# Issuing one of four small row DMAs from ScalarE's queue, and six stack DMAs without a gap

## What is computed

```python
logits = einsum('bhqd,bhkd->bhqk', q, k) * scale      # causal mask added
attn = softmax(logits)
out = einsum('bhqk,bhkd->bhqd', attn, v)
for l in range(2):
    x = x + attention(ln(x))
    x = x + (token_moe, seq_moe)[l](ln(x))
```

## Time and profile before

| what | us |
|---|---|
| median of 3 runs | 1255.74 (1254.58 to 1256.5) |
| profiled execution, its own time | 1253.16 |
| its span, first to last instruction | 1251.4 |
| TensorE busy in the span | 1060.6 (85%) |
| VectorE busy | 980.6 (78%) |
| ScalarE busy | 792.0 (63%) |
| GpSimd busy | 685.8 (55%) |

### The profile page before, as it was taken

How to read it: one execution, slowest core, us unless ns; L and a number is a source line. 1 busy time by engine, 2 the same in 40 slices (tenths; PEclk the granted TensorE clock), 3 DMA queues, 4 the chain that set the end, 5 groups by cost and what they waited for, 6 DMA issues and landing times. The chain is left out here.

```text
span 1251.4 us, 37899 instructions
## 1 busy us (share of the span) xinstructions
PE 1060.6 (85%) x10453; PEld 789.4 (63%) x10453; DVE 980.6 (78%) x2919; ACT 792.0 (63%) x1908; POOL 685.8 (55%) x1018
## 2 busy tenths in 40 slices
PE   1788999999999999999369997388889889989997
PEld 0565666666666666666269997255656556658986
DVE  3678999999998898899547765368888998876665
ACT  1566777777777767776158886256666666754554
POOL 3345555556656777776723333566676676532332
PEclk9999999999999999999679999589999899989999
DMA  5232111111111221121122222243311212100000
GB/s 144 86 110 78 50 38 42 51 52 53 53 40 45 68 66 52 55 66 43 36 72 67 69 67 74 57 116 99 85 53 53 64 39 67 53 2 10 23 18 21
DMA packets 118053, 73.07 MB, mean 58 GB/s; under 512 B 8384, under 2 KB 112960, under 8 KB 117952
## 3 DMA queue, kind: packets, MB, share of 16 engines
q1 hardware_dynamic: 99296, 53.11, 15.3%
q10 hardware_dynamic: 14560, 10.35, 3.0%
q0 software_dynamic: 4096, 8.40, 2.1%
HBM read 21.68 MB, written 11.60 MB: 27 GB/s over the span
## 5 line engine op out<-in xcount | busy, mean ns | idle before, releaser
L617 DVE TENSOR_REDUCE negm<-bank 128x2 f32<-128x512 f32 (+1 forms) x576 | 389.3, 679 | 82.0 <-PE bank L309 57.0
L505 ACT ACTIVATE prob<-bank 128x512 f32<-128x512 f32 x576 | 339.6, 595 | 127.1 <-PE bank L331 88.8
L898 POOL TENSOR_SCALAR_AFFINE_SELECT prob<-prob 128x512 f32<-128x512 f32 x384 | 248.6, 649 | 172.6 <-ACT prob L505 170.7
L350 PE MATMUL bank<-prob,vaug 128*32 128x256 f32 (+1 forms) x3072 | 168.6, 338 | 4.1 <-ACT oT L511 3.3
L1217 POOL COPY w_job<-w_s 128x512 f32 x104 | 69.1, 665 | 153.4 <-PE bank L1186 152.6
L317 PE MATMUL bank<-stack 126*128 126x256 bf16 x768 | 151.8, 279 | 0.0
L336 PE MATMUL bank<-stack 128*128 128x256 bf16 x768 | 150.8, 278 | 0.9 <-ACT prob L505 0.9
L1208 ACT ACTIVATE prob<-bank,b_job 128x128 f32<-128x128 f32 (+1 forms) x416 | 131.8, 400 | 17.2 <-PE bank L1186 9.9
L1197 PE MATMUL bank<-w_job,prob 128*128 128x128 f32 x1088 | 139.0, 276 | 2.5 <-issue 1.6
L1197 PEld LDWEIGHTS bank<-w_job,prob 128*128 128x128 f32 x1088 | 131.3, 192 | 6.4 <-issue 5.3
L350 PEld LDWEIGHTS bank<-prob,vaug 128*32 128x32 f32 x3072 | 81.5, 110 | 80.7 <-issue 48.9
(11 more groups left out here) (181 smaller groups left out, 2122.0 us busy)
## 6 DMA issues: line engine op xcount, KB each, us to landing
stack<-parts SPq DMA_DIRECT2D x288, 128.0 KB
w_s<-e_w ACTq DMA_DIRECT2D x32, 256.0 KB, 3.0
oT<-x_routed SPq DMA_DIRECT2D x72, 64.0 KB, 1.7
y_routed<-oT SPq DMA_DIRECT2D x36, 128.0 KB, 1.9
stack<-mT SPq DMA_DIRECT2D x192, 4.0 KB
out<-x_all SPq DMA_DIRECT2D x16, 128.0 KB, 1.8
b_all<-e_b ACTq DMA_DIRECT2D x2, 512.0 KB, 8.4
x_routed<-hk,x_at POOLq DMA_INDIRECT x64
```

Of the source, the lines that this page charges most:

```text
L350: m = nc.tensor.matmul(o, w, (prob0, prob1)[kb][:, g % 2, h], start=kb == 0, stop=kb == 1, skip_group_check=True)
L505: nc.scalar.activation(o, s, ACT.Exp, scale=SCALE).then_inc(exp_done, 1)
L617: nc.vector.tensor_reduce(o, s, AX.X, ALU.max, negate=True).then_inc(max_done, 1)
L898: nc.gpsimd.affine_select(out=t, in_=t, compare_op=ALU.is_ge, fill=0.0, base=0, pattern=[[0, HG], [1, P]], channel_multiplier=-1).then_inc ...
```

## The change

In slot 2 of phases two and three, the row of group 1 is issued by ScalarE's queue, right after the second of the three exponentials of the slot, and SP issues the six stack DMAs of the next sample in a run. In phase one nothing is moved. The waits of the row (`mT_sb`, `sT_ps`) go with it. All other rows stay with SP.

```diff
+        def row(eng, i, g):
+
+            eng.wait_ge(mT_sb, 4 * i.v + g + 1)
+            alone(eng)
+            need(eng, sT_ps, 12 * (i.v - 2) + 3 * g + 3)
+            alone(eng)
+            eng.dma_start(stack[SHIFT:P, i.par, HG * g:HG * (g + 1), 0],
+                          mT[:, g % 2, :]).then_inc(row_dma[g % 2], 16)
+
@@ act_slot
             if ie:
                 act_exp(ie, ge, 1)
+            if k == 2 and im and im.phase > 0:
+                row(act, im, gm)
             if k == 1 and nxt:
                 act_part(nxt)
@@ sp_slot
+            by_act = k == 2 and im and im.phase > 0
             if k == 2 and nxt:
-                sp_stack(nxt, range(0, 2))
-            if im:
-                sp.wait_ge(mT_sb, 4 * im.v + gm + 1)
-                alone(sp)
-                need(sp, sT_ps, 12 * (im.v - 2) + 3 * gm + 3)
-                alone(sp)
-                sp.dma_start(stack[SHIFT:P, im.par, HG * gm:HG * (gm + 1), 0],
-                             mT[:, gm % 2, :]).then_inc(row_dma[gm % 2], 16)
-            if k == 2 and nxt:
-                sp_stack(nxt, range(2, 6))
-            if k == 3 and nxt:
-                sp_stack(nxt, range(6, TERMS))
+                sp_stack(nxt, range(TERMS if by_act else 2))
+            if im and not by_act:
+                row(sp, im, gm)
+            if k == 2 and nxt and not by_act:
+                sp_stack(nxt, range(2, TERMS))
```

## The result

| | median us | runs | ratio to before, 95% interval |
|---|---|---|---|
| before | 1255.16 | 1250.76 to 1256.5 (4) | 1 |
| changed | 1279.7 | 1274.61 to 1283.44 (4) | 1.0195 [1.0165, 1.0224] |

The change makes the kernel 2% slower, 24.5 us by the medians. The forecast was 1250.3. The profiled execution of the changed kernel took 1280.74 us, its span is 1279.0.

What follows compares the result with a forecast made beforehand. In phases two and three neither TensorE nor VectorE is full; they wait for each other. The terms 2.4 + 3.0 + 0 = 5.4 us gave 1255.74 - 5.4 = 1250.3 us, range 1244.5 to 1257.5.

Steps and rivals of the forecast that it cites:

- rival C: Phases two and three: the unbroken stack burst delays the row; 1265.3 us at a flight of 3.4 us; chance 0.12.
- When the row goes out: Row behind ScalarE's second exponential: leaves 0.3 us earlier in phase two; a 2.4 us flight holds even for late exponentials.
- the late second exponential: Exponential at 954.29 after late score matmuls, row needed at 957.43: with a flight of 2.4 us, 0.6 us left.
- I read the difference as queueing that a row on another queue mostly escapes: Row behind two stack DMAs: 3.74 us in phase three's sample with loads, 2.36 in the ordinary one; another queue mostly avoids this.
- The row leaves SP: ScalarE's extra issue of 0.34 to 0.66 us fits in its 0.83 us idling in the slot: priced at nothing.
- What it is worth in phase two: Earlier row in phase two: taken as 0, since VectorE sets the sample's length; at most 4.9 us.
- What it is worth at 835.86: Phase three sample with expert loads: row leaves earlier, removing 2.81 us of idling; gain 2.4 us, bounds 1.0 and 2.8.
- SP issues six in a run: SP's issue gap goes, so TensorE's stack waits in phases two and three shrink: 3.0 us, bounds 0 and 3.9.
- rival A: The transfers, not SP's issue, set the stack's landing, so the gap is worth 0: 1254.7 us, chance 0.24.
- a sign of being wrong: TensorE's granted clock in phase three, 0.96 before, moving by more than a hundredth would count against the forecast.

Runs made afterwards that it cites:

- e15: Kernel before, but the row goes out on SP behind three stack DMAs, with three behind it: 1273.95 us, ratio 1.0160.
- e5: Changed kernel, but SP issues two stack DMAs, waits until ScalarE has issued the row, then issues four: 1262.4 us, ratio 1.0066.
- e11: Changed kernel, but SP issues three stack DMAs, waits until ScalarE has issued the row, then issues three: 1273.9 us, ratio 1.0153.
- e4: Kernel before, plus an extra 4 KB DMA on ScalarE's queue in slot 2, where the change has the row: 1260.0 us, ratio 1.0043.
- e6: Kernel before, plus an extra 4 KB DMA on ScalarE's queue in slot 3: 1261.1 us, ratio 1.0063.
- e7: The change in phase three alone, phase two as in the kernel before: 1264.6 us, ratio 1.0100.
- e8: Kernel before, row on SP, but SP holds the four stack DMAs behind the row until it has landed: 1309.2 us, ratio 1.0440.
- e2: Kernel before, but the row goes out on SP behind four stack DMAs, with two behind it: 1311.4 us, ratio 1.0465.

## Why the prediction was wrong

The forecast (faster by 5.4 us) failed, and rival C, to which I gave 0.12, came: the row is delayed, L331 waits for it in nearly every sample, and the stages grow by what it waits.

- **"When the row goes out"** is the step that failed. Its first half held in phase two: 0.25 us behind the second exponential instead of 0.1, so 0.15 us sooner than from SP instead of 0.3. The second half, "with a flight of 2.4 us this holds", didn't: 3.5 in phase two. I took the flight from a row that had two stack DMAs ahead and moved the row, without asking what would be ahead of it then. In the kernel before, SP's own queue keeps the third stack DMA behind the row. Afterwards SP issues the third 1.38 us after the first, and ScalarE's row leaves at 1.69: it has become the fourth DMA instead of the third, and 128 KB more are ahead of it. e15, e5 and e11 show that this place is what counts, on whichever of the two queues. For the late second exponential, 954.29 in the prediction, I had counted 0.6 us to spare. In the changed kernel nine rows of phase three are that late, have four stack DMAs ahead, and land at 5.8 to 6.2 us.
- **"I read the difference as queueing that a row on another queue mostly escapes"** fell with it. The Trainium skill's rule (DMA: Bandwidth & Descriptors, Issuing engines are not separate DMA queues), that DMAs of all issuing engines run on the same DMA engines and that a second issuer saves no more than the time of initiating, agrees with e5, e11 and e15. The interleaving that the prediction quotes with it didn't help the row: its packets on ScalarE's queue moved only when the stack DMAs issued earlier were nearly through. I had weighed the rule for one sample of phase three, at 0.7 us; in the other 30 samples it changes the sign.
- **"The row leaves SP", at nothing:** not quite right. The third exponential starts up to 0.41 us late, L534 still idles, but an extra DMA of this size costs 5 to 7 us in e4 and e6, which I can place only in part.
- **"What it is worth in phase two", 0:** the slack was smaller still than the 0.2 us that I read. The landing grew by 0.9 to 1.0 us, and the sample by 13.8/15 = 0.92.
- **"What it is worth at 835.86", 2.4:** the mechanism held (e7); measured 1.8, since the stack landed 8.7 us after its first DMA, where I had allowed 8.0.
- **"SP issues six in a run", 3.0:** the issue became 0.7 us shorter (5.02 to 4.33). In the changed kernel the stack waits went from 0.6 + 3.3 to 1.8 in all (the 0.6 is gone). But TensorE was late by then for the row, which hides such waits. The landings that the traces record for the stack show the term by itself: the last of the six goes out 0.94 us sooner after the first in phase two and 1.0 us in phase three, but all have landed only 0.1 us sooner (7.78 us after the first issue for 7.90, medians) and 0.3 us (7.64 for 7.95). I had taken 0.7 from two samples of phase one. With 0.9 us of transfer for each 128 KB against 0.67 us of issue, the premise of rival A was right: the transfers set the pace. The Trainium skill (DMA: Bandwidth & Descriptors, Why a DMA increments its semaphore by 16 and not by 1) has such copies on 8 of 16 engines; the busy share of 0.50 to 0.57 in the run, after a first stretch of 0.7, agrees. By the same rule the row, two partitions wide at its destination, would run on 2 engines, the lowest-numbered, which the stack copies use too. The packets of 4 bytes in the trace, 8 for each stack DMA and 2 for each row, agree with the numbers; no run here shows which engines move what.
- **Rival C's price** was low. At the measured flight (3.5 in phase two, 3.6 as the median of all) its sum gives (3.6 - 2.9) x 30 - 5.4 = 15.6 us, 1271. The 5.4 us it subtracts didn't arrive in full, and some 4 us may have come with the clock: in phase three 2.5, and 1.6 in the expert jobs between, where TensorE's busy time rose from 177.85 to 179.47 us at 0.87 instead of 0.88. Over the window of the earlier trace rows in phase three the clock went from 0.96 to 0.94 (840 to 1140 afterwards), which the prediction had named as a sign of being wrong. Rival C's mechanism was half right: not the four "poured in" while the row flies (e8), but the third, and in nine samples the fourth, which get ahead of it.

**Left open:** the 0.5 us that come on top in four samples of phase two with the row on ScalarE's queue; where e6 loses its time; whether bytes or packets ahead set the delay; and some 5 us between the changed kernel and e11 or e15, whose intervals overlap with its own. In the profiled executions e11 is the shorter one in phase three alone (288.4 us against 298.6), e15 by 2.8 us in each of the two phases. In phase three both keep the fourth stack DMA behind the row, but their clock is higher there too (0.97 and 0.94 over the stage, against 0.90), and no run separates the two.

## What to carry to other kernels

A small, urgent DMA that shares its way with large ones is as late as the large ones issued ahead of it make it, on either of the two queues measured here (SP's and ScalarE's). Before moving it to another queue, write down what will be ahead of it then: its old queue may have been what held the large ones back. A gap in a queue's issue that looks like waste may be exactly that protection.

## What the runs showed of the hardware

- The landing grows in steps with the 128 KB DMAs ahead: about 3.0 us after the first with one (3.2 on SP), 4.2 to 4.3 with two, 5.2 with three, 6.1 with four. It was the same on SP's and ScalarE's queue, but for the 0.5 us above (with four: e2 on SP, the nine samples of phase three in the changed kernel on ScalarE's), and with two ahead it was 4.2 both for a row that left at 1.67 and for one at 2.23.
- Six such DMAs issued in a run, in 3.4 us from the first issue to the last instead of 4.4, had landed only 0.1 to 0.3 us sooner.
- DMAs issued behind the row on the same queue, up to 512 KB, didn't delay it (e8 against the kernel before).
- A 4 KB DMA took as long to issue (0.65 us) as one of 128 KB (0.67).
